# Building a graph's count matrix inside the later attention passes, with the projection's constant column rewritten

## What is computed

```python
x = _layernorm(x + _L0_gnn_ref(x, src, dst, ...))   # attention: softmax over a node's edges, weighted sum of feat[src]
x = _layernorm(x + _L1_gnn_ref(x, edge_index, edge_attr_128, ...))  # edge rows summed by src, then an MLP
x = _layernorm(x + _L2_gnn_ref(x, ...))             # three attention convolutions, each with a batch norm
x = _layernorm(x + _L3_gnn_ref(x, src, dst, ...))   # five times:
#   agg = jax.ops.segment_sum(h[src], dst, num_segments=N);  rst = h + agg;  two linear layers, three batch norms
```

## Time and profile before

| | us |
|---|---|
| median of 3 runs | 8978.68 (8977.43 to 8986.32) |
| profiled execution | 8993.16 |
| its span | 8991.8 |
| `positions` | 309.5 |
| `source_sums` | 388.8 |
| `adjacency_steps` | 99.3 |
| `adjacency` | 704.7 |
| first attention pass | 676.9 |
| later passes | 1082.5, 1084.8, 1084.5 |

### The profile page before, as it was taken

One profiled execution on the slowest core, in us unless ns is written; L12 is line 12 of the kernel. 1 busy time (PEld: TensorE's weight loads), 2 busy tenths in 40 slices (PEclk: granted clock), 3 DMA queues, 4 the chain that ended last, 5 costly groups with the idle time before them and its releaser, 6 DMA issues. The chain is left out here.

```text
span 8991.8 us, 135316 instructions
## 1 busy us (share of the span) xinstructions
PE 5567.6 (62%) x30230; PEld 4477.6 (50%) x30231; DVE 4739.3 (53%) x12204; ACT 4511.6 (50%) x8872; POOL 4381.9 (49%) x4415
## 2 busy tenths in 40 slices
PE   1621111756776886466665666656666498998986
PEld 1610001742225774355554555645555487776865
DVE  3820000559997877555554555555555645445455
ACT  1038886008996774444444444444444444444344
POOL 1877777737771000477774777747777300000000
PEclk8555555878888998787886888778888799999998
DMA  3433334855665441233332333323333286676764
GB/s 102 120 101 105 107 105 111 233 136 183 211 211 160 135 131 46 65 84 85 84 84 70 85 84 84 85 69 84 84 84 84 57 264 199 217 251 199 252 212 154
DMA packets 724312, 1173.04 MB, mean 130 GB/s; under 512 B 118807, under 2 KB 546470, under 8 KB 723608
## 3 DMA queue, kind: packets, MB, share of 16 engines
q1 hardware_dynamic: 366644, 612.04, 22.0%
q0 software_dynamic: 150784, 336.22, 15.6%
q10 hardware_dynamic: 206628, 221.92, 8.7%
HBM read 955.51 MB, written 216.73 MB: 130 GB/s over the span
## 5 line engine op out<-in xcount | busy, mean ns | idle before, releaser
L1204 POOL DMA_INDIRECT ring<-gat_rows,src_idx x2496 | 2417.8, 969 | 1004.4 <-issue 1001.3
L1324 PE MATMUL ps<-ring,xT_b 128*128 x8192 | 1410.3, 325 | 1236.1 <-ACT xT_b L1410 1230.7
L1324 PEld LDWEIGHTS ps<-ring,xT_b 128*128 128x128 f32 x8192 | 1219.0, 228 | 1448.8 <-issue 1446.9
L1402 ACT ACTIVATE xT_a<-xT_a,state 128x514 f32<-128x514 f32 x1024 | 740.1, 723 | 1824.0 <-SPq L1176 1293.5
L1814 PE MATMUL ps<-wide,features 128*128 128x504 f32 (+1 forms) x6370 | 1438.8, 384 | 18.2 <-DVE features L1714 16.2
L1814 PEld LDWEIGHTS ps<-wide,features 128*128 128x128 f32 x6370 | 1156.8, 189 | 252.3 <-DVE wide L1682 17.4
L1372 DVE CUSTOM_DVE_ANT_0 xT_a<-ps,mask,xT_a 128x512 f32<-128x512 f32 x1024 | 767.0, 749 | 607.5 <-PE ps L1315 488.8
L697 POOL DMA_INDIRECT by_src<-ring,state x832 | 803.4, 966 | 255.9 <-issue 253.0
L1054 POOL TENSOR_TENSOR x_nodes<-x_nodes,last_state 128x1280 f32<-128x1280 f32 x3 | 9.9, 3312 | 1792.2 <-SPq L227 1792.2
L1315 PE MATMUL ps<-ident,s_col 128*128 128x128 f32 x4096 | 747.0, 315 | 187.5 <-DVE s_col L1339 122.5
L1419 ACT ACTIVATE xT_b<-xT_a,neg 128x514 f32<-128x514 f32 x1024 | 741.6, 724 | 33.1
(11 more groups left out here) (383 smaller groups left out, 8761.4 us busy)
## 6 DMA issues: line engine op xcount, KB each, us to landing
xT_a<-adjacency SPq DMA_DIRECT2D x245, 756.0 KB
dl_all<-dloc_rows ACTq DMA_DIRECT2D x1052, 128.0 KB, 3.1
xT_b<-adjacency SPq DMA_DIRECT2D x150, 812.0 KB
xT_a<-adjacency SPq DMA_DIRECT2D x95, 812.0 KB
adjacency<-xT_b ACTq DMA_DIRECT2D x294, 252.0 KB
ring<-by_src SPq DMA_DIRECT2D x52, 1040.0 KB
ring<-gathered SPq DMA_DIRECT2D x208, 260.0 KB
ring<-in_edge_attr SPq DMA_DIRECT2D x103, 512.0 KB
```

Source lines behind the costliest of these rows:

```text
L1204: pool.indirect_dma_start(ring[:, o:o + RC], None, table[:, :], bass.IndirectOffsetOnAxis(src_idx[:, t * W + u:t * W + u + 1], 0)).then_in ...
L1324: m = pe.matmul(bank(BO + v % 2, R), pw[v % 4][:, w * P:(w + 1) * P], ring[:, w * RC:][:, bass.ds(look(SLOT, u - 7), R)], start=w == 0, st ...
L1402: act.activation(um[u % 4], sm[u % 8], ACT.Identity, bias=S[:, ER:][:, bass.ds(look(BC, u), 1)]).then_inc(q["act_a"], 1)
```

## The change

The stretch `adjacency` is gone. Its steps, padded to 1536 and put in two streams that each run through the keys in order, are done inside the three later attention passes, two (one of each stream) in each of the 256 steps of a pass. DVE makes the one-hot tiles for step n+1 behind its other work of step n (`make_nodes`). PE, behind the turn of step n-5, runs two matmuls for each stream (`add_counts`): the first takes in what the stream has so far (the last evicted tile, times the identity, or times zero where a new key begins), the second adds this step. ACT evicts both sums at the end of its step (`evict_counts`) and stores the tiles of the step before to `counts` (`store_counts`), at a place that is a dump unless the key ends there. The score banks in these passes are two, no longer four. The one window which both streams share is mended after the last pass.

`positions` counts bins by 50 compares and matmuls over whole rows, and ranks by 50 more rounds. The gathers for the first pass are stored in pairs of tiles and split anew: tiles 0 to 13 in `positions`, to 79 in `source_sums`, to 95 in `adjacency_steps`; tiles 96 to 207 are gathered in the first pass into the ring. Since the staging buffers now hold one-hot tiles in the passes, their constant column is written again in front of each projection. `blk_rows` and its store are gone from the set-up.

```diff
-FIRST = 32
-EARLY = 78
-TABLES = 90
+FIRST = 14
+EARLY = 80
+STORED = 96
+assert STORED % RT == 0
 RUN = 16
 NV = -(-(W * T) // RUN)
-NH = 5
-HELD = 3
+NH = 3
+PAIR = 2
+HELD = 1
...
+STREAMS = 2
+PASSES = 3
+AK = STREAMS * PASSES * K
+assert AK >= AT + NKEY - 1
 AJ = -(-AK // P)
-AKP = AJ * P
-KEYJ = -(-NKEY // P)
+assert AJ * P == AK
+PER = STREAMS * K
+DROP = NB * P * NWIN
...
+            def count_bins():
+                for b in range(BINS):
+                    dve.tensor_scalar(hit[b], block, float(b), None, ALU.is_equal).then_inc(q["eq"], 1)
+                for b in range(BINS):
+                    pe.wait_ge(q["eq"], b + 1)
+                    for h in range(2):
+                        m = pe.matmul(PS[:, h * 512:h * 512 + HT], strip[:, 64 - b:192 - b],
+                                      hit[b][:, h * HT:(h + 1) * HT], start=b == 0, stop=b == BINS - 1)
                 m.then_inc(q["product"], 1)
...
+            def rank_bins():
+                s.wait(pe)
+                for b in range(BINS):
+                    if b >= 4:
+                        pe.wait_ge(q["summed"], b - 3)
+                    for h in range(2):
+                        to = PS[:, b % 4 * 1024 + h * 512:b % 4 * 1024 + h * 512 + HT]
+                        pe.matmul(to, earlier, hit[b][:, h * HT:(h + 1) * HT], start=True, stop=False)
+                        m = pe.matmul(to, choose[:, b:b + 1].to_broadcast([P, P]), pieces[:, h * HT:(h + 1) * HT],
+                                      start=False, stop=True)
+                    m.then_inc(q["masked"], 1)
+                for b in range(BINS):
+                    dve.wait_ge(q["masked"], b + 1)
+                    if b:
+                        dve.wait_ge(q["summed"], b)
+                    dve.tensor_tensor(two(best), two(best), halves(b % 4), ALU.max).then_inc(q["summed"], 1)
+                dve.wait_ge(q["summed"], BINS)
+                dve.tensor_scalar(pos[:, :], best, ABOVE, None, ALU.subtract)
...
+            s.together((sp, lambda: sp.dma_start(step_rows[0:1, :], keep_i), 16),
+                       (sp, lambda: sp.dma_start(step_rows[1:2, :], at_i), 16),
+                       (sp, lambda: sp.dma_start(joint[:, :], same[:, AK // 2:AK // 2 + 1]), 16),
+                       (sp, lambda: sp.dma_start(joint_at[:, :], first_i), 16))
...
+            s.together(*[(sp, lambda c=c: sp.dma_start(of_steps[c, :, :], XTa[:, 3072 + c * AK:3072 + (c + 1) * AK]), 16)
+                         for c in range(2)], (dve, lambda: dve.tensor_copy(window_ids, node_ids[:, 0:WD])))
...
+            first, pairs = begin // PAIR, (end - begin) // PAIR
+            assert begin % PAIR == 0 and end % PAIR == 0
+            each = PAIR * W
...
+            for n in range(pairs):
                 h = n % NH
                 if n >= NH:
                     pool.wait_ge(q[f"kept{h}"], 16 * (n // NH))
-                for u in range(W):
-                    i = (begin + n) * W + u
+                for u in range(each):
+                    i = (first + n) * each + u
                     pool.indirect_dma_start(held[h][:, u * RC:(u + 1) * RC], None, gat_rows[:, :],
                                             bass.IndirectOffsetOnAxis(src_idx[:, i:i + 1], 0)
                                             ).then_inc(q[f"rows{h}"], 16)
...
                 for g in range(RT):
-                    if not first:
-                        sp.wait_ge(q["product"], free[g])
-                    sp.dma_start(ring[:, g * W * RC:(g + 1) * W * RC],
-                                 gathered[bass.ds(it * RT + g, 1), :, :].rearrange("a p c -> (a p) c")
-                                 ).then_inc(q[f"rows{g}"], 16)
-
-            load(0, True)
-            with sp.Fori(1, TITER) as it:
-                load(it, False)
-
-            with pool.Fori(0, TITER) as it:
-                for g in range(RT):
-                    pool.wait_ge(q[f"rows{g}"], it * 16 + 16)
-                    pool.sem_inc(q["tiles"], 1)
+                    if (not first or g >= RT - SOON) and (not last or g < RT - SOON):
+                        sp.wait_ge(q["product"], sp.snap(regs[g], min_val=1, max_val=K))
+                        later = g + SOON
+                        if whole if later < RT else whole_next:
+                            load(tile_of(it + later // RT, later % RT), later % RT)
+                        else:
+                            sp.sem_inc(q["room"], 1)
+                    landed(it, g, whole)
...
+            for t in range(STORED, T):
+                g = t % RT
+                pool.wait_ge(q["room"], t - STORED + 1)
+                for u in range(W):
+                    o = (g * W + u) * RC
+                    pool.indirect_dma_start(ring[:, o:o + RC], None, gat_rows[:, :],
+                                            bass.IndirectOffsetOnAxis(src_idx[:, t * W + u:t * W + u + 1], 0)
+                                            ).then_inc(q[f"got{g}"], 16)
+            return [(f"got{g}", 16 * W * (TITER - stored)) for g in range(RT)]
...
+            def load_steps():
+                for c, to in enumerate((src_steps, dst_steps)):
+                    act.dma_start(to[:, 0:PER], of_steps[c, :, bass.ds(turn * PER, PER)]).then_inc(q["load"], 16)
+                act.dma_start(keep_tab[:, 0:PER], step_rows[0:1, bass.ds(turn * PER, PER)]).then_inc(q["load"], 16)
+                act.dma_start(at_tab[:, STREAMS:STREAMS + PER], step_rows[1:2, bass.ds(turn * PER, PER)]
+                              ).then_inc(q["load"], 16)
+                for tab, o in ((keep_tab, PER), (at_tab, STREAMS + PER)):
+                    dve.memset(tab[:, o:], 0)
+                dve.memset(at_tab[:, 0:STREAMS], 0).then_inc(q["memset"], 1)
+                for eng in (pe, act, dve):
+                    eng.wait_ge(q["load"], 64)
+                    eng.wait_ge(q["memset"], 1)
...
+            def make_nodes(n, u, have):
+                if have(2):
+                    dve.wait_ge(q["added"], n * STREAMS - STREAMS)
+                dve.tensor_tensor(node1[u % 4].rearrange("p (x n) -> p x n", n=P), node_row,
+                                  src_steps[:, u * STREAMS:][:, bass.ds((n - u) * STREAMS, STREAMS)]
+                                  .rearrange("p (x a) -> p x a", a=1).to_broadcast([P, STREAMS, P]), ALU.is_equal)
+                for x in range(STREAMS):
+                    m = dve.tensor_scalar(node2[u % 2 * STREAMS + x], window_ids,
+                                          dst_steps[:, u * STREAMS + x:][:, bass.ds((n - u) * STREAMS, 1)],
+                                          None, ALU.is_equal)
+                m.then_inc(q["eq"], 1)
+            def add_counts(n, u, have):
+                pe.wait_ge(q["eq"], n + 1)
+                if have(1):
+                    pe.wait_ge(q["out"], n * STREAMS)
+                if u % 8 == 0:
+                    keep_at[:] = rows_of(pe, 2 * U, 8 * STREAMS, keep_tab, n, P)
+                for x in range(STREAMS):
+                    pe.matmul(tile(x), carry[:, bass.ds(keep_at[u % 8 * STREAMS + x], P)], evicted[(u - 1) % 2 * STREAMS + x],
+                              start=True, stop=False)
+                    pe.matmul(tile(x), node1[u % 4][:, x * P:(x + 1) * P], node2[u % 2 * STREAMS + x],
+                              start=False, stop=True).then_inc(q["added"], 1)
+            def evict_counts(n, u, have):
+                for x in range(STREAMS):
+                    act.wait_ge(q["added"], n * STREAMS + x + 1)
+                    if have(2):
+                        act.wait_ge(q[f"st{u % 2 * STREAMS + x}"], (n - u) * 8 + u // 2 * 16)
+                    act.activation(evicted[u % 2 * STREAMS + x], tile(x), ACT.Copy).then_inc(q["out"], 1)
+            def store_counts(n, u, later):
+                for x in range(STREAMS):
+                    act.wait_ge(q["out"], n * STREAMS + x + 1)
+                    act.dma_start(counts[bass.ds(store_at[later % 2 * STREAMS + x], P, step=NWIN), :],
+                                  evicted[u % 2 * STREAMS + x]).then_inc(q[f"st{u % 2 * STREAMS + x}"], 16)
...
             def pe_body(n, u, have, look):
                 if have(0):
                     pe.wait_ge(q["s_ready"], n + 1)
-                    if have(4):
-                        pe.wait_ge(q["masked"], n - 3)
+                    if have(wide_scores):
+                        pe.wait_ge(q["masked"], n + 1 - wide_scores)
                     for w in range(W):
-                        m = pe.transpose(bank(BS + u % 4)[:, w * P:(w + 1) * P],
+                        m = pe.transpose(spread(u)[:, w * P:(w + 1) * P],
                                          s_col[u % 4][:, w:w + 1].to_broadcast([P, P]), ident[:, :])
                     m.then_inc(q["bcast"], 1)
...
+                if have(0) and not streamed:
+                    add_counts(n, u, have)
...
+                    if not streamed:
```

(17 more changed lines are left out.)

403 lines of the change are left out of this document (180 added, 223 removed).

## The result

| | before | after |
|---|---|---|
| median of the runs | 8978.8 us | **8461.5 us** (8459.5 to 8472.7) |
| profiled execution, span | 8991.8 us | 8458.1 us |

The ratio is **0.9425, 95% interval 0.9408 to 0.9441**: 5.7% faster. The forecast was 8404 us, 58 us too low, inside its range of 8340 to 8640.

A forecast was written before the change was run, and what follows sets the result against it. GpSimd's gathers were taken to bound a later pass. The count stage's -704.7 us and `positions`' -192, against +196 for the first pass, +81 for later passes and smaller terms, gave -575: 8404 us, range 8340 to 8640.

The forecast's parts named there:

- First pass, +196: First attention pass: 112 tiles gathered into the ring from 280 us on make it 873 us in place of 676.9.
- `adjacency_steps`, +32: Stretch `adjacency_steps`: 64 gathers, 8 stores and two awaited new stores make it 131 us in place of 99.3.
- Later passes, +27: Three later attention passes: GpSimd still sets them, and the count work adds 27 us to each, 81 in all.
- 0.14 for the register loads of each 16 steps: Later passes, ACT's step: 0.14 us for a block's register loads, within a sum of 3.75 to 3.9 us.
- the 7 us of backlog: Later passes: an allowance of 7 us a pass for backlog because the engines' margin is thin.
- The 13 us for slower gathers: Later passes: DVE's new compares slow GpSimd's gathers, 13 us a pass.
- `source_sums`, +2: Stretch `source_sums`: 264 gathers and 33 stores take 364 to 372 us, under its 388.8; 0 to +10, taken +2.
- `positions`, -192: Stretch `positions`: compares, matmuls and maxima replace the scans, 118 us in place of 309.5.
- Small terms: Set-up -4 us, mend of the shared window +12, constant column and small copies before three passes +3.
- (b): Rival, later passes: PE stays at 1.2 GHz, a step takes 5.3 us, a pass +287 over forecast, 9265 us; chance 0.05.
- (c): Rival, later passes: the compares lock GpSimd out, +173 us a pass over forecast, 8923 us; chance 0.03.
- (a): Rival, later passes: the engines' chain takes over from GpSimd, 4.5 us a step, pass 1192, total 8653 us; chance 0.24.

The follow-up runs named there:

- before_again: The kernel before, unchanged, executed and traced once more: `source_sums` took 389.8 us at a granted clock of 0.85.
- no_stores: The changed kernel with all four gathers a tile, the two count stores per step left out: gathers of 1.016 us, a later pass 1124 us.
- no_node1: no_stores with the compare of 256 columns run only in the first four steps of a pass: the pass stays at 1123 us.

## Why the prediction was right, and where its terms were off

**The bound was read rightly.** GpSimd's four gathers a tile set the later pass of before, and count work under them is nearly free: 41 us where 426 would be its bare price. The stage of 704.7 us went whole.

**The total is closer than its terms.** The later passes, `source_sums`, the first pass and `adjacency_steps` came out 81 us above their terms, `positions` and the small terms 40 us below theirs. That these cancelled to 41 is luck. The other 16 of the 58 us are the step from a profiled execution to the median: 14.5 was taken off, and after's profiled execution lies 2 us under its median.

**First pass, +196 for +202, and `adjacency_steps`, +32 for +35:** right, by their own steps. In after the gathers of the first pass start 285 us into it (280 predicted), run for 570 (570) and leave an end of 23 (23).

**Later passes, +27 for +40 each.** The step that was mis-sized is "0.14 for the register loads of each 16 steps" in ACT's sum. That is ACT's own load spread over a block, and ACT's own lies beside the others; at the end of a block one load of PE and two of DVE stand in a row, 6.4 us, and 1.5 more come in the middle, about 0.5 us a step. The rest of ACT's sum, 3.61, measured 3.74. The engines' bound is then 1107 us, where 3.85 us a step and 50 us of start and end make 1035. So the 7 us of backlog were too few: with 7 for the last steps, 14 were given, and the end of the pass is 24 us longer. The 13 us for slower gathers were 17.5, 10 and 13.5 in the three passes, which is near. Their mechanism was held to be the number of compares; it is what a gather meets when it starts, and for how long that runs.

**`source_sums`, +2 for +35.** "Under the 388.8" treated the stretch as fixed as long as GpSimd is done first. GpSimd was done 39 us ahead, and yet the stretch grew: 18 us at an equal clock, about 9 of them by the gathers, and 17 with a lower one. The cause of the lower clock stays open.

**`positions`, -192 for -221.** The term was taken at the low clock, as the stretch had run before, though the text gave the high level's number beside it: "where DVE's maxima (about 1.0 us each) set 52". The granted clock there is 0.92, and the 50 maxima took 51 us. With its own figures for the high level, 21 us for counting (100 x 0.206) and 52 for the maxima, the prediction's sum gives 89, what was measured. The clock of a stretch was carried over to a stretch with other work in it.

**Small terms.** The mend took 9.0 us against 3.6 for what stood there before, +5 for the +12. The set-up gave -4.2 for -4. The three stretches with the projections took 0.5, 1.3 and 1.2 us more, +3 for +3, though one such stretch differed by 0.8 us between before and before_again. The rest of the balance is in the last layer, which took 6.4 us less; why, no run shows.

**Rivals.** (b) didn't come near: the passes were granted 0.91 to 0.93, more than the 0.81 of before. (c) by its worst case was out, as the earlier trace rows said. (a) was half true: the engines' own pace, 1107 us, did come level with GpSimd's 1103, but far under the 1192 at which (a) was priced.

## What to carry to other kernels

Work can be hidden under a queue that is full, up to where the engines' own pace meets it; that pace is to be summed per block of the loop, with the register loads of all engines on a timeline, since those of engines that wait for each other can stand in a row. When two bounds meet, take one away in an experiment before easing it in the kernel: here leaving out the stores, 182 us of the engines' pace, brought nothing. An idle start of the bounding queue, as in the first pass, was worth 149 us.

## What the runs showed of the hardware

- A gather that starts beside a DVE instruction with two inputs of 256 columns or more in SBUF, or beside a `tensor_scalar` compare with one, ends about 0.82 us after that instruction, in place of 0.944 after its own start. Beside the masked maximum (one input in PSUM, 0.75 us) it is not delayed: none of 176 in a pass of before.
- What one costs goes with its length. `tensor_scalar` compares of 0.35 us made 7.6 ns a gather in no_stores; one `tensor_tensor` of 1008 columns and 1.20 us in their place made 173, and the mean gather 1.188 us in place of 1.016.
- Taking such an instruction away (no_node1) didn't shorten the mean gather: another was met more often.
- Loading registers from SBUF took 1.97 us for 32 on ACT, 1.87 for 28 on DVE, 1.11 for 16 on PE, 0.31 for four on ACT.
- The granted clock of one and the same stretch of the changed kernel went from 0.78 to 0.86 between executions, and its length from 430 to 407 us.
